# An addition moved ahead of the query's rotary sum, and smaller moves beside it, in an attention and expert kernel

## The reference

```python
x  = L0_attn_x
xn = _layernorm(x)
x  = x + attn(xn, W_Q, W_K, W_V, W_O, b_Q, ...) + ffn(xn, ln1_w, ..., wsd)

# attn: 16 heads of 128, causal, with biases
q, k, v = x @ W_Q + b_Q, x @ W_K + b_K, x @ W_V + b_V
out = einsum(softmax(causal(q k^T / sqrt(128))) v, W_O) + b_O

# ffn: rms norm, then 16 query heads and 4 key/value heads with rotary embedding
q = q * cos + rotate_half(q) * sin ;  k = k * cos + rotate_half(k) * sin
x = resid + o @ wo
# then 32 experts, the 4 best of each row by probs + bias_e, and one shared expert
probs = softmax(xn2 @ gate_w.T); _, sel = top_k(probs + bias_e, 4)
return resid2 + moe_y + shared
```

## Time and profile before

| | |
|---|---|
| median of 3 runs | 758.54 us (757.89 to 759.56) |
| the profiled execution | 761.44 us, span 759.6 us |
| busy: PE, PE loads, DVE, ACT, POOL | 733.5, 658.1, 576.7, 514.9, 492.0 us |
| mean granted clock of TensorE | 0.998 of full speed |

### The profile page before, as it was taken

One profiled execution on the slowest core, in us unless ns is written; L12 is line 12 of the kernel. 1 busy time (PEld: TensorE's weight loads), 2 busy tenths in 40 slices (PEclk: granted clock), 3 DMA queues, 4 the chain that ended last, 5 costly groups with the idle time before them and its releaser, 6 DMA issues.

```text
span 759.6 us, 14674 instructions
## 1 busy us (share of the span) xinstructions
PE 733.5 (97%) x4700; PEld 658.1 (87%) x4700; DVE 576.7 (76%) x1732; ACT 514.9 (68%) x1274; POOL 492.0 (65%) x559
## 2 busy tenths in 40 slices
PE   7899998999899999999999999999999999999997
PEld 4688897988788888988987888999989999999996
DVE  6888977797878887676788567767767776777675
ACT  4777776687777776677446565766666766676762
POOL 5767777787867786335476565466655866666565
PEclk9999999999999999999999999999999999999999
DMA  6001000000011299200111443377876877667735
GB/s 197 23 2 35 15 22 15 22 15 22 15 50 35 72 315 274 58 15 16 42 29 43 119 144 103 102 177 181 192 181 162 199 170 174 157 146 163 154 36 166
DMA packets 102725, 76.99 MB, mean 101 GB/s; under 512 B 6951, under 2 KB 101499, under 8 KB 102651
## 3 DMA queue, kind: packets, MB, share of 16 engines
q1 hardware_dynamic: 91890, 63.41, 29.3%
q0 software_dynamic: 10608, 12.61, 10.5%
q10 hardware_dynamic: 152, 0.06, 0.0%
HBM read 51.36 MB, written 24.69 MB: 100 GB/s over the span
## 4 chain that ended last, share of the span: by engine, by line
PE 70%; DVE 8%; ACT 7%; POOL 7%; issue 3%; DMA 2%; SPq 2%; ACTq 0%; another core or an unknown queue 0%; DVEq 0%; POOLq 0%
PE j L946 20%; PE zb L946 10%; PE ob L946 10%; PE s L946 9%; PE t L1105 8%; POOL probs L739 3%; PE j L1050 3%; ACT probs L1291 2%; PE ob L1050 2%; DVE rope_sum L1651 2%; PE zb L1050 2%; DVE probs L1604 1%; DVE probsT L1619 1%; ACT rope_swapped L1332 1%; ACT rope_swapped L1331 1%
## 5 line engine op out<-in xcount | busy, mean ns | idle before, releaser
L739 POOL TENSOR_SCALAR probs<-probs,inv_sum 128x256 f32<-128x256 f32 (+1 forms) x235 | 144.8, 631 | 140.7 <-DVE inv_sum L1610 135.5
L1291 ACT ACTIVATE probs<-probs,neg_max 128x128 f32<-128x128 f32 (+3 forms) x256 | 143.3, 560 | 101.3 <-DVE neg_max L1604 77.1
L946 PE MATMUL s<-k_heads,q_heads 128*128 128x256 f32 (+2 forms) x576 | 137.9, 360 | 2.6 <-issue 1.4
L1604 DVE CUSTOM_DVE_ANT_0 probs<-s,mask 128x128 f32<-128x128 f32 (+3 forms) x256 | 120.7, 486 | 17.8 <-PE s L946 11.2
L831 POOL DMA_INDIRECT moe_sum_dram<-late,slot_tokens x63 | 103.1, 1637 | 26.6 <-ACT late L1379 13.9
L1619 DVE TENSOR_TENSOR probsT<-t,probsT 128x384 fp32r<-128x384 f32 x191 | 101.1, 549 | 19.8 <-ACT probsT L1306 11.9
L1306 ACT ACTIVATE probsT<-t 128x384 fp32r<-128x384 f32 x191 | 90.4, 489 | 26.0 <-PE t L1105 20.3
L1105 PE MATMUL t<-ident,probs 128*128 128x128 f32 x638 | 95.3, 277 | 9.9 <-POOL probs L739 7.1
L946 PEld LDWEIGHTS s<-k_heads,q_heads 128*128 128x128 f32 x576 | 90.7, 189 | 7.9 <-DVE neg_max L1604 2.1
L1105 PEld LDWEIGHTS t<-ident,probs 128*128 128x128 f32 x638 | 73.5, 142 | 18.6 <-POOL probs L739 13.0
L946 PE MATMUL zb<-probsT,v_heads 128*128 128x512 f32 (+2 forms) x351 | 69.3, 341 | 1.4 <-DVE probsT L1619 0.6
(11 more groups left out here) (295 smaller groups left out, 1661.0 us busy)
## 6 DMA issues: line engine op xcount, KB each, us to landing
x_slots_dram<-mask SPq DMA_DIRECT2D x1, 8480.0 KB, 40.1
late<-x_slots_dram SPq DMA_DIRECT2D x32, 265.0 KB
late<-in_L_ffn_weg_dram SPq DMA_DIRECT2D x63, 128.0 KB
late<-in_L_ffn_weu_dram SPq DMA_DIRECT2D x63, 128.0 KB
late<-in_L_ffn_wed_dram SPq DMA_DIRECT2D x63, 128.0 KB
moe_sum_dram<-mask SPq DMA_DIRECT2D x2, 1152.0 KB, 6.9
raw_qk<-in_L_ffn_wq_dram SPq DMA_DIRECT2D x16, 128.0 KB, 2.3
raw_o<-in_L_ffn_wo_dram SPq DMA_DIRECT2D x8, 256.0 KB
```

What stands on the lines that cost most here:

```text
L739: pool.tensor_scalar(piece, piece, rinv[:, u % 2, i:i + 1], 1.0, ALU.mult, ALU.mult).then_inc(p_norm, 1)
L946: m = pe.matmul(dst, lhs(a), rhs(b), start=first and i == 0, stop=last_ and i == 2, skip_group_check=skip)
L1291: act.activation(piece, piece, ACT.Exp, bias=nmax[:, u % 2, i:i + 1], scale=-1.0, accum_out=rsum[:, u % 2, i:i + 1]).then_inc(e_done, 1)
L1604: ve.tensor_tensor_reduce(pr[:, u % 2, P_OFF[i]:P_OFF[i] + width], bS[i % 2][:, 0:width], mask_t[:, S - width:S], INV_SCALE, BIG, ALU.add, ...
```

## The change

`add_out` stands in front of the query's `rope_sum` in steps 2 to 29. The two additions of `b_O` move from steps 9 and 17 to 30 and 31. The scatters keep their order and number (32) but are grouped otherwise, and both parts of a step wait for scores of the next unit. In the router, three of the five steps of the prefix sum and five small operations leave the front of steps 39 and 40 for later places in the same steps. The split of query weights 2 of group 5 moves from step 38 to step 37. Two row scalings on ACT stand ahead of `z_part` in step 35. SP issues the raw loads one step later, ahead of that step's expert weights.

```diff
-    SENT = {HALF + 8: (5, 2), HALF + 9: (4, 4), HALF + 10: (4, 4), HALF + 11: (4, 4), HALF + 12: (1, 0)}
+    SENT = {HALF + 8: (5, 0), HALF + 9: (4, 3), HALF + 10: (4, 4), HALF + 11: (4, 3), HALF + 12: (5, 0)}
...
         if 4 <= s < 8 and a + 1 < UNITS // GS:
-            found.append((f"Q{s - 4}", a + 1))
+            found += [(f"Q{q}", a + 1) for q in range(4) if s - 4 == (1 if (a, q) == (HALF // GS, 2) else q)]
...
                         slot_rows(r + i)
+                if n_of(r) == HALF + 2 * GS + 1:
+                    loads(2 * GA - 1, 1, GA - 1, kinds[:5])
+                if n_of(r) == HALF + 2 * GS + 4:
+                    loads(2 * GA - 1, 1, GA - 1, kinds[5:])
                 for i in (3, 4):
                     if r + i < PAIRS:
                         expert_weights(r + i)
-                if n_of(r) == HALF + 2 * GS:
-                    loads(2 * GA - 1, 1, GA - 1, kinds[:5])
-                if n_of(r) == HALF + 2 * GS + 3:
-                    loads(2 * GA - 1, 1, GA - 1, kinds[5:])
...
                 if n in SENT:
-                    if part:
-                        pool.wait_ge(z_mm, n + 1)
-                    elif n < HALF + 12:
-                        pool.wait_ge(s_mm, TB * (n + 2))
+                    pool.wait_ge(s_mm, TB * (n + 2) if part else TB * (n + 1) + 1)
...
-                if n in (GS + 1, 2 * GS + 1):
+                if n in (HALF - 2, HALF - 1):
                     pool.wait_ge(bc_in, 32)
                     pool.wait_ge(ln_step, LN["xn", NT - 1])
-                    half = NT // 2
-                    tiles = accB[:, (n // GS - 1) * half:n // GS * half, :]
+                    half, b = NT // 2, n - (HALF - 2)
+                    tiles = accB[:, b * half:(b + 1) * half, :]
...
                     normalise(n, (3,))
+                    scale_rows(SCALED.get((n, 1), ()))
                     z_part(n, it)
...
-                    scale_rows(SCALED.get((n, 1), ()))
...
                     silu(n, 4)
+                    route_2(n, 0)
                     if nxt:
                         invert(n + 1, 3, it)
+                    route_2(n, 1)
...
                     route_1(n)
+                    route_2(n, 2)
...
                 invert(n + 1, 3, it)
+                if 2 <= n:
+                    add_out(n, it)
                 rope_sum(chs[0], it)
                 for ch in v_last:
                     chunk(ch, it)
-                if 2 <= n:
-                    add_out(n, it)
...
                     shift_add(2)
-                    for s in (4, 8, 16):
-                        shift_add(s)
-                    then(ve.tensor_tensor(first_e, run[1][:, E:2 * E], blocks_e, ALU.subtract))
-                    then(ve.tensor_scalar(first_e, first_e, float(P), 1.0, ALU.mult, ALU.add))
...
+            def route_2(n, part):
+
+                if n == RANKS + 1 and part == 0:
+                    shift_add(4)
+                    shift_add(8)
+                if n == RANKS + 1 and part == 1:
+                    shift_add(16)
+                if n == RANKS + 1 and part == 2:
+                    then(ve.tensor_tensor(first_e, run[1][:, E:2 * E], blocks_e, ALU.subtract))
+                    then(ve.tensor_scalar(first_e, first_e, float(P), 1.0, ALU.mult, ALU.add))
+                if n == RANKS + 2 and part == 0:
                     then(ve.tensor_scalar(ended, run[1][:, E:2 * E], bn_t[:, 0:1], None, ALU.is_le))
                     then(ve.tensor_reduce(et_t[:, 0:1], ended, AX.X, ALU.add))
+                if n == RANKS + 2 and part == 1:
                     ve.tensor_scalar(et_t[:, 0:1], et_t[:, 0:1], float(E - 1), None, ALU.min).then_inc(et_done, 1)
```

## The result

The changed kernel takes 751.57 us in the median of seven runs (750.40 to 755.52), the kernel before 758.50 beside it (seven runs, 756.83 to 759.56). The ratio is 0.9937 with a 95% interval of 0.9913 to 0.9961, so the change makes it 0.6% faster. The forecast was 753.2 with a range of 747.0 to 758.0.

The account below looks back on a forecast made before the run. PE, busy 97% of the span, bounds the kernel, leaving some 26 us of idle to win. Terms sum to -6.15 us against the profiled 761.44, taken as -5.3 against the median 758.54: 753.2, range 747.0 to 758.0.

Parts of the forecast that it names:

- the swap: Rotary steps, add_out ahead of rope_sum: shorter POOL scalings, but a later mask delays PE's block 2; +2.9 us.
- the expert rows: Step 45: last scatter later behind step 44's key/value weights, PE's wait grows 1.2 us; counted 0 with the scatter gain.
- the theory of the idle: Scatter steps: ACT and DVE idle towards the end of eight scatters in a row; shorter series save 1.2 us.
- Bias: b_O additions leave steps 9 and 17: 2.2 us each plus 1.7 for low clock, -6.1; new place costs nothing.
- Rival A: Rotary steps: the bank's wait is absorbed, term -3.9 in place of +2.9, time 746.4; chance 0.18.
- Rival B: Rotary steps: rope_sum's delay reaches PE in every step, also behind the out-projection; +10.4, time 760.7; chance 0.10.
- Row scaling: Step 35: two scalings fit in ACT's idle ahead of z; PE's wait of 0.37 at 355.78 goes, 0.4 us.
- step 39: Router: small operations leave DVE's front ahead of masks 2 and 3; gain 0.6 us, bounds 0 and 1.3.
- Step 40: Router: 0.56 us leaves the front, about PE's wait at 415.67; gain 0.55 us.
- Rival C: Scatter and router moves only shift waits, last scatter costs 5 us; 759.4, no change; chance 0.10.
- Raw loads: SP issues them later, so step 50's rows leave earlier; PE's wait of 1.35 goes, -1.4 us, bounds 0 and 1.5.

Follow-up runs that it names:

- e2: Kernel before with only the two b_O additions moved to steps 30 and 31: 751.86 us, ratio 0.9935.
- e1: Kernel before with only add_out put ahead of the query's rope_sum in steps 2 to 29: 758.23 us, ratio 1.0028.
- e6: e3 with ACT's half of z ahead of its half of the query in two rotary steps of four: 748.66 us, ratio 0.9842.
- e4: Changed kernel with add_out behind the rotary sum and chunks again, as before: 753.34 us, ratio 0.9966.
- e10: e3 with the router's additions, the weight split of step 37 and the row scaling at their old places: 755.04 us, ratio 0.9909.
- e12: e3 run once more, on the third chip: 753.62 us, ratio 0.9878.
- e3: Changed kernel with the scatter series and their waits as in the kernel before: 748.13 us, ratio 0.9902.
- e9: e3 with the raw loads back at their old place, behind the expert weights: 753.07 us, ratio 0.9901.
- e13: e6 run once more, on the third chip: 750.50 us, ratio 0.9842.
- e11: The changed kernel itself run again, on the third chip: 755.18 us, ratio 0.9902.
- e7: Kernel before with add_out ahead of the rotary sum and the b_O additions in steps 30 and 31: 756.09 us, ratio 0.9940.

## Why the prediction was right, and where it was wrong

The direction, and the term that carries it, were right. The time came out 1.6 us below the forecast, inside the range, and in part that was luck: the swap had the wrong sign, the expert rows were costed too low, the theory of the idle was wrong, and these errors ran against each other.

**Bias: right.** -6.1 forecast, -5.6 measured in the three stretches; 2.2 us each taken, 2.06 measured for each (2.19 and 2.16 in e2, without the swap), and 1.5 for the low clock (1.7 taken). The clock was at half for 3.4 us there, from 124.6 to 128.0; the 1.8 us of the forecast are what that costs and not its length. That term hangs on the execution: behind e1's waits of 2.46 and 2.24 the clock stayed up. e2 shows that it alone gives the whole gain of the first comparison. It was costed at nothing at the new place, and there POOL's 2.41 us fit.

**`add_out` ahead of `rope_sum`: the mechanism right, the size wrong, and with it the sign.** The step said that a round "loses 0.5 us in place of winning 0.56". It won 0.13 (34.47 to 34.34). Each link was found: blocks 2 and 3 on POOL take 1.41 us and not 1.90, PE's block 2 waits for DVE's mask in steps 14 and 15 (marked 0.24 in the first), e6 shows whose order it is. The sizes along the chain were too large. Counted from the start of POOL's block 2 (146.59 after, 150.50 before), `rope_sum` ends 0.6 us later than before and not 0.8, and DVE's half of z starts 0.6 later and not 0.8. The mask starts 0.2 later and not 0.5, since the short idle times ahead of the copies and of the mask took up 0.4 and not 0.3. PE's block 2 follows the mask, 0.2 later and not 0.5. One part of this is that durations were added up end to end. In the rows after, the addition of 0.69 us starts at 147.12 and the next operation at 147.72, and `rope_sum` of 0.81 at 147.72 is followed at 148.45: each neighbour starts 0.08 to 0.09 us before the duration is over. So the term of +2.9 measured -0.8 in the profiled pair, and -0.5 by e4. Rival A (-3.9) lies nearly as far off on the other side, and its reason was false: the bank's wait is there. Rival B, the slower one, fell: the steps with an out-projection in between show no marked wait.

The Trainium skill (SBUF — State Buffer, section "SBUF: two separate sides") makes the shared port pair of VectorE and GpSimd a lock held for a whole instruction. The trace after agrees: with `add_out`, which reads PSUM, beside them, the two scalings take 1.41 us. And `rope_sum`, which starts 0.28 us before they end, ends 0.53 us behind them (148.53 against 148.00). In the kernel before, the stretched sum of the earlier trace rows ends at 194.52, 0.54 us behind the sine product that ran beside it on POOL:

```profile
192.69 1.29 POOL L840 TENSOR_TENSOR rope_swapped<-rope_swapped,rope 128x512 f32<-128x512 f32 x1
```

In both cases the sum is done some 0.5 us behind POOL's end, however early it began, and that, not the 0.7 us of its duration alone, is what the forecast should have added.

**Row scaling and router: right in the sum, by terms that were not.** The wait of 0.37 at 355.78 cost 0.9 and not 0.4. PE's four transposes there took 1.25 us from the first pair's start to the next piece (355.02 to 356.27), where the changed kernel's take 0.36 (348.71 to 349.07). A mark counts from the modelled end of the piece before, which lies past the next start in an unbroken sequence; the loss is the difference of starts. In step 39 the same: 0.84 marked, and the stretch is 1.04 shorter. The key's half behind it (0.30 marked at 405.62) gave another 0.44: from the transposes of unit 40 to the next piece it was 1.40 us (404.22 to 405.62) and is 0.96 (395.99 to 396.95). So step 39 won 1.5 where 0.6 was taken, over its bound of 1.3. Step 40 won nothing of its 0.55: the wait for ACT's block is still there (0.52 marked at 407.08, 0.44 before), and by starts it is 0.08 longer. What its small moves gave by themselves no run tells, since e10 undoes all of them at once.

**Scatters and expert rows: the step that failed.** It had two halves. "I take half of 2.4 us away" rested on the idle standing behind eight scatters in a row. e12 against e3 shows it coming and going with one and the same kernel. In the profiled pair the idle that is gone makes 3.55 us, on the first chip nothing, on the third perhaps 2. "The weights can start up to 3.8 us earlier, which leaves 1.2" left out what the weights themselves wait for: PE's last product with the old ones. The 4.62 us of idle at 448.74 says so. They start 1.75 earlier, 3.4 remain, and the measured term is +3.3 to +3.5 against e3 (+2.7 in the profiled pair) and not +1.2. My bound of 5.1 held it; the value in it was taken by counting a queue and not looking at the releaser behind it. Rival C's mechanism (the last scatter comes late, a wait over 2 us) did happen, and was paid for by the other terms.

**Raw loads: right in direction.** -1.4 taken, -1.5 in unit 51 of the pair; units 52 and 53 took 0.5 more, but unit 53 has the same 16.50 in e1 and e2 with the loads at the old place, so most of that is no price of the move. Over all profiles unit 51 gains 0.9 on average, 0.4 to 1.0 by e9, so 1.4 was near the upper end.

**The sum.** Of -11.0 us in the profiled pair, 3.55 are the idle that varies. What is left, -7.5, stands against -4.95 forecast for the same terms: the swap (3.7 too dear), the row scaling (0.5), the router (0.25) and the rest (0.5) on the one side, the expert rows (1.5), the bias (0.5) and the loads (0.4) on the other. That these cancel as far as they do is luck and not insight. The forecast for the median is off by less, 1.6, because the profiled execution of the kernel after stands 1.2 below its own median, where that of the kernel before stood 2.9 above.

## What to carry to other kernels

Try the move with the clearest marked wait alone first. Here it gave the whole gain of the first comparison, while the regrouping that rested on idle without a cause cost 3 us. A step moved earlier in a queue gains only up to its next releaser, so for each thing that "can now start earlier" look up what frees its operands, its output buffer above all. Where a wait stands on an engine with a ready operation behind the waiting one, turning the two round (e6) can be worth more than moving work between stages. And one profiled pair can carry several microseconds of idle that no edit made: before an unexplained gap is given a cause, look whether the same kernel shows it in a second execution.

## What was not expected of the hardware

- The idle of units 43 and 45 has a place but no cause that these runs show. ACT is held in front of copies of transposes (2.88 and 3.05 us in e12, released by no instruction of this core that the trace names), only in some executions; it stays open. A rival is the loading of instructions: a packet of some 16 KB on a DMA queue for instructions moves within 2 us behind the transposes of unit 42, inside the first of these idle times. But it does so in all fourteen profiles, also in the five without the idle (the changed kernel's own and e1 to e4), so that its presence alone is not the cause; whether it comes late in the others no view shows.
- The granted clock falls to half, 1.2 GHz, for 3.4 us at a time, in e12 once for 6.8. It did so at the end of PE's idle of 2.29 us before or just behind it, and so at 2.67 in e13, 3.33 in e11 and 3.35 in e12. It did not behind 3.29 in the changed kernel's own profile, 3.16 in e4, or 2.46 and 2.24 in e1. And in five profiles (e2, e4, e7, e10, e12) it fell at the 32 narrow matmuls of the router's logits in step 36, in e4 and e12 with no idle of PE marked ahead. In e12 that window has a mean of 0.83 at full PE busy time, and the unit takes 17.89 in place of 14.73:

```profile
350.00:370.00 20.00, 20.00 (x118) 18.11 (x117) 11.71 (x48) 9.18 (x24) 8.30 (x12) 0.83 0.14 40
```

  The times of a kernel spread with it: 750.40 to 755.52 for the changed kernel, 747.31 to 749.48 for e3. A long wait goes with more low clock: a mean clock of 0.995 or less stands in 33 of 76 runs of the kernels in which PE waits over 2 us for the bias or for the rows (before, e1, e4, e11 and the changed kernel), and in 5 of 50 runs of the others; on the first chip alone it is 22 of 42 and 0 of 12. So such a wait costs more than its length. It is not the only cause, since e12 without it spreads from 751.60 to 757.88.
- The same kernel before had medians of 757.21, 761.20 and 762.03 us on three chips, a difference as large as most terms here. Of times, only ratios to the kernel before were compared between them.
